# A routing pass folded into the unrolled feed-forward loop before it, and a regrouped head and tail of the state space stage

## What is computed

```python
y = groupnorm_complex(gate_loop(k, v, q, a), gn_scale, gn_bias) * silu(g)
y = (y @ Wo).real
x1 = layernorm(x + y, ln1_scale, ln1_bias)
out = x1 + (gelu(x1 @ W1 + b1) @ W2 + b2)
x = x + layernorm(out, ln2_scale, ln2_bias)
...
xn = layernorm(x)                              # router of layer 0
logits = xn @ gate_kernel                      # 64 experts
weights, selected = top_k(logits, 2)           # softmax over the two
sort_idx = argsort(selected.reshape(-1))       # rows of an expert go together
...
h = rmsnorm(layernorm(x))                      # layer 1
x_, z = split(h @ in_proj.T); xc = silu(causal_conv(x_))
dt, B, C = split(xc @ x_proj.T); dt = softplus(dt @ dt_proj.T + bias)
h_t = exp(dt * A) * h_(t-1) + (dt * xc) * B    # 512 channels x 16 states
x = x + ((sum over states of h_t * C) + D * xc) * silu(z) @ out_proj.T
```

## Time and profile before

| | us |
|---|---|
| median of 3 runs | 3226.64 (3224.76 to 3228.54) |
| the profiled execution | 3244.09 |
| its span, first to last instruction | 3242.3 |
| PE busy | 2644.0 (82%) |
| DVE busy | 1915.0 (59%) |
| POOL busy | 1381.8 (43%) |
| ACT busy | 1100.5 (34%) |

### The profile page before, as it was taken

One profiled execution on the slowest core, in us unless ns is written; L12 is line 12 of the kernel. 1 busy time (PEld: TensorE's weight loads), 2 busy tenths in 40 slices (PEclk: granted clock), 3 DMA queues, 4 the chain that ended last, 5 costly groups with the idle time before them and its releaser, 6 DMA issues. The chain is left out here.

```text
span 3242.3 us, 36222 instructions
## 1 busy us (share of the span) xinstructions
PE 2644.0 (82%) x12202; PEld 1809.4 (56%) x12202; DVE 1915.0 (59%) x3395; ACT 1100.5 (34%) x1766; POOL 1381.8 (43%) x865
## 2 busy tenths in 40 slices
PE   6772599754999999997488888988878776997998
PEld 3331366543999999996133333433433334666997
DVE  6999687362221221222789999999899994331211
ACT  6775122100111111111445545556465430221111
POOL 0000244335333333332059688697786851112332
PEclk9886799955999999998689998989989887998999
DMA  3000100012899999886200010110000101116996
GB/s 112 0 1 0 44 13 19 13 41 70 322 325 321 327 325 324 320 310 215 96 26 33 26 40 27 38 35 27 33 33 33 33 26 33 40 39 220 350 346 240
DMA packets 95181, 395.13 MB, mean 122 GB/s; under 512 B 21366, under 2 KB 48518, under 8 KB 72544
## 3 DMA queue, kind: packets, MB, share of 16 engines
q1 hardware_dynamic: 73472, 351.46, 30.9%
q0 software_dynamic: 21600, 42.37, 3.6%
HBM read 364.94 MB, written 39.29 MB: 125 GB/s over the span
## 5 line engine op out<-in xcount | busy, mean ns | idle before, releaser
L1327 POOL TENSOR_TENSOR ss_h<-ss_h,ss_cs 128x2048 f32<-128x2048 f32 x128 | 579.1, 4526 | 78.3 <-DVE ss_h L1693 70.3
L1407 PE MATMUL ss_y<-ss_h,all_ident 128*128 128x512 f32 x1024 | 525.8, 662 | 52.2 <-POOL ss_h L1327 52.0
L1176 DVE TENSOR_TENSOR experts_in<-experts_sil,experts_pU 128x512 f32<-128x512 f32 x176 | 120.9, 687 | 646.6 <-PE experts_pU L1120 612.8
L1693 DVE TENSOR_TENSOR_SCAN ss_h<-ss_da,ss_c_h,ss_dbu 128x512 f32<-128x512 f32 x384 | 470.7, 1268 | 7.4 <-ACT ss_da L1553 0.6
L1407 PEld LDWEIGHTS ss_y<-ss_h,all_ident 128*128 128x128 f32 x1024 | 215.3, 214 | 329.2 <-issue 263.1
L1553 ACT ACTIVATE ss_da<-ss_dt,ss_decay 128x512 f32<-128x512 f32 x512 | 326.7, 711 | 119.1 <-DVE ss_h L1693 69.0
L1686 DVE TENSOR_TENSOR ss_dbu<-ss_dtx,ss_bB 128x1024 f32<-128x1024 f32 x256 | 314.5, 1228 | 62.5 <-PE ss_bB L1397 36.0
L1120 PE MATMUL experts_pG<-experts_xt,experts_wa 128*128 128x128 f32 x2816 | 346.8, 277 | 0.9 <-DMA experts_wa<-in_w_all 0.9
L1120 PE MATMUL experts_pU<-experts_xt,experts_wa 128*128 128x128 f32 x2816 | 344.4, 276 | 0.0
L1129 PE MATMUL experts_pY<-experts_wa,experts_in 128*128 128x256 f32 x1408 | 332.7, 379 | 0.0
L1120 PEld LDWEIGHTS experts_pG<-experts_xt,experts_wa 128*128 128x128 f32 x2816 | 331.8, 193 | 1.3 <-ACT experts_xt L1146 1.1
(11 more groups left out here) (318 smaller groups left out, 3675.5 us busy)
## 6 DMA issues: line engine op xcount, KB each, us to landing
experts_wa<-in_w_all SPq DMA_DIRECT2D x176, 1536.0 KB
ss_cs<-ss_c_rows SPq DMA_DIRECT2D x64, 512.0 KB, 3.6
moe_rows<-route_xn SPq DMA_DIRECT2D x16, 512.0 KB
ss_h<-moe_ys SPq DMA_DIRECT2D x5, 1024.0 KB, 8.4
all_x<-in_x SPq DMA_DIRECT2D x8, 512.0 KB, 9.1
gf_xb<-in_x SPq DMA_DIRECT2D x8, 512.0 KB, 3.9
moe_rows<-all_x SPq DMA_DIRECT2D x8, 512.0 KB, 3.0
experts_xr<-moe_rows,moe_token POOLq DMA_INDIRECT x176
```

The source lines that it names most:

```text
L1176: nc.vector.tensor_tensor(IN[t.two][:].rearrange("p f t -> p (f t)"), SIL[t.two][:], pU[t.two][:], ALU.mult)\
L1327: pool.tensor_tensor(h[:], h[:], CS[q % 2][:, n % GROUP].unsqueeze(1).to_broadcast([P, CI, BT]), ALU.mult)\
L1407: mm = pe.matmul(y[:, c], ident[:], H[(b * N + n) % RING][:, c], start=(n == 0), stop=(n == N - 1))
L1693: ins = V.tensor_tensor_scan(H[(b * N + n) % RING][:, c], DA[(b * N + n) % AHEAD][:, c], DBU[:, c % 2], first, ALU.mult, ALU.add)
```

## The change

gate_ffn and the routing of layer 0 become one function, gate_ffn_route, unrolled in Python over NB + 3 = 11 steps in place of the hardware loops. In step i the first half of the feed-forward works on block i, the second half on block i-1, the router's rows, transposes and logits on block i-2, and its choice, ranks, slots and scatters on block i-3. The router's PSUM tiles pL and pR lie inside pW, the output of the W2 matmuls. The router's row statistics are found block by block. The closing part of the routing (number of tiles, owners, list gather, weights) is the same.

In state_space, block 0's Silu is taken chunk by chunk from PSUM with the bias, and x_proj takes each chunk as it comes; row_stats does its two inverse square roots in one chain over a two-row tile, and its call for blocks 1 to 7 stands before split_bc(0). At the end the last state's product is cut in two halves, PE adds it up chunk by chunk, DVE does skip and gate by chunk, and the output projection accumulates over the chunks in four regions of PSUM (LAST) that are free by then.

```diff
-def gate_ffn(nc, g, X, YS, SG, SUMS, ident):
...
+def gate_ffn_route(nc, g, X, YS, SG, SUMS, gate, r, ident):
...
+        pL, pR = (pW[:, 2 * n:2 * n + 2].rearrange("p t d -> p (t d)") for n in range(2))
+        pLt = pL[:, 0:TPB * E].rearrange("p (t e) -> p t e", e=E)
+        pRt = pR[:, 0:(TPB + 1) * E].rearrange("p (t e) -> p t e", e=E)
...
+        STEPS = range(NB + 3)
+        inside = lambda b: 0 <= b < NB
...
+                def enlist(b):
+                    wait(pool, "slots_ready", b + 1)
+                    for j in range(TPB):
+                        for k in range(K):
+                            pool.indirect_dma_start(lists, bass.IndirectOffsetOnAxis(ap=SL[b % 2][:, j, k:k + 1], axis=0),
+                                                    entry[:, b * TPB + j, k], None).then_inc(listed[b % 2], 16)
+
+                for i in STEPS:
+                    if inside(i):
+                        x1(i)
+                    if inside(i - 3):
+                        enlist(i - 3)
+                    if inside(i - 1):
+                        out(i - 1)
+                for h in range(2):
+                    pool.wait_ge(listed[h], LISTED * (NB // 2))
+                wait(pool, "list_done", 1)
...
+                def ffn_down(i):
+                    wait(pe, "h_free", i * FC + FC)
+                    wait(pe, "w2_read", i * TPB)
+                    wait(pe, "slots_ready", i - 1)
...
+                def route_turn(b):
+                    wait(pe, "rxn_done", b * TPB + TPB)
+                    wait(pe, "rxt_done", b * KD)
...
+                def logits(b):
+                    wait(pe, "rxt_done", b * KD + KD)
+                    wait(pe, "index_done", b)
+                    wait(pe, "w2_read", min(b + 2, NB) * TPB)
...
+                def ranks(b):
+                    wait(pe, "onehot_done", b * TPB + TPB)
+                    wait(pe, "slots_ready", b)
+                    wait(pe, "w2_read", min(b + 2, NB) * TPB)
...
+                for i in STEPS:
+                    if inside(i):
+                        wo(i)
+                    if i == 1:
+                        wait(pe, "loaded", LOADED)
+                        wait(pe, "gate_loaded", 16)
+                        wait(pe, "consts", 1)
+                    if inside(i - 3):
+                        ranks(i - 3)
+                    if inside(i - 1):
+                        ffn_up(i - 1)
+                    if inside(i - 2):
+                        route_turn(i - 2)
+                    if inside(i - 1):
+                        ffn_down(i - 1)
+                    if inside(i):
+                        turn(i)
+                    if inside(i - 2):
+                        logits(i - 2)
...
+                for i in STEPS:
+                    if inside(i - 1):
+                        gelu(i - 1)
+                    if inside(i - 2):
+                        copy_route(i - 2)
+                    if inside(i):
+                        copy_xt(i)
...
+                def route_rows(b):
+                    wait(dve, "out_done", b + 1)
+                    wait(dve, "rxt_raw", b - 1)
+                    if b > 1:
+                        dve.wait_ge(rows_stored[b % 2], 16 * (b // 2))
+                    normalise(lambda j: X[:, b * TPB + j], RXN[b % 2], "rxn_done", 1e-5)
...
+                z(0)
+                for i in STEPS:
+                    if inside(i - 3):
+                        choose(i - 3)
+                    if inside(i):
+                        first(i)
+                    if inside(i - 3):
+                        place(i - 3)
+                    if inside(i - 2):
+                        route_rows(i - 2)
+                    if inside(i + 1):
+                        z(i + 1)
+                    if inside(i - 1):
+                        second(i - 1)
...
+        LAST = [Q[:, 0:D], bB[:, 0:D], DBU[:, 0, 0:D], DBU[:, 1, 0:D]]
...
-                        wait(pool, "scanned", (b * N + n + 1) * 2)
+                        wait(pool, "scanned", (b * N + n + 1) * 2 - (1 if not prep and n == N - 1 else 0))
+                        if not prep and n == N - 1:
+                            break
...
-                gate(NB - 1)
+                last, row = H[(NB * N - 1) % RING], CS[(NB * GROUPS - 1) % 2][:, GROUP - 1].unsqueeze(1).to_broadcast([P, 2, BT])
+                pool.tensor_tensor(last[:, 0:2], last[:, 0:2], row, ALU.mult).then_inc(s["last_product"], 1)
+                wait(pool, "scanned", NB * N * 2)
+                pool.tensor_tensor(last[:, 2:4], last[:, 2:4], row, ALU.mult).then_inc(s["last_product"], 1)
...
-                    wait(pe, "xc_done", b + 1)
+                    wait(pe, "xc_done", b)
                     if b > 1:
                         wait(pe, "out_done", (b - 1) * 2)
-                    project(Q[:], WX, 0, XC[b % 2], CI).then_inc(s["xp_raw"], 1)
+                    for k in range(CI):
+                        if b == 0:
+                            wait(pe, "xb_done", k + 1)
+                        mm = pe.matmul(Q[:], WX[:, k], XC[b % 2][:, k], start=(k == 0), stop=(k == CI - 1))
+                    mm.then_inc(s["xp_raw"], 1)
...
-                add_up(NB - 1, N - 1)
-                out_part(NB - 1, 0)
-                out_part(NB - 1, 1)
+                for c in range(CI):
+                    wait(pe, "last_product", c // 2 + 1)
+                    pe.matmul(y[:, c], ident[:], H[(NB * N - 1) % RING][:, c], start=False, stop=True).then_inc(s["last_sum"], 1)
+                wait(pe, "z_done", NB * CI)
+                wait(pe, "dbu_done", NB * N * 2)
+                wait(pe, "scanned", NB * N * 2)
+                for c in range(CI):
+                    wait(pe, "yz_done", (NB - 1) * CI + c + 1)
+                    for j in range(TPB):
+                        mm = pe.matmul(LAST[j], DTX[(NB - 1) % 2][:, c, j * P:(j + 1) * P], WO[:, c], start=(c == 0), stop=(c == CI - 1))
+                        if c == CI - 1:
+                            mm.then_inc(s["out_raw"], 1)
...
-                    A_(XC[b % 2][:, c], bank(b, c), ACT.Identity, bias=conv_b[:, c:c + 1]).then_inc(s["xb_done"], 1)
+                    A_(XC[b % 2][:, c], bank(b, c), ACT.Silu if b == 0 else ACT.Identity, bias=conv_b[:, c:c + 1])\
+                        .then_inc(s["xb_done"], 1)
...
-                    A_(XC[b % 2][:], XC[b % 2][:], ACT.Silu).then_inc(s["xc_done"], 1)
+                    if b > 0:
+                        A_(XC[b % 2][:], XC[b % 2][:], ACT.Silu).then_inc(s["xc_done"], 1)
...
-                    v, d, q, t = var[:, a:b], rstd[:, a:b], rms[:, a:b], tmp[:, a:b]
-                    norm_stats(nc, pre, lambda j: X[:, a + j], stats[:, a:b], mv[:, a:b], d, t, 1e-5, var=v)
...
+                    v, r, w, d, t = VARS[:, :, a:b], ROOTS[:, :, a:b], TMP2[:, :, a:b], rstd[:, a:b], tmp[:, a:b]
...
+                    pre.mark(V.tensor_scalar(v[:, 0], mv[:, a:b, 1], 1.0, 1e-5, ALU.mult, ALU.add))
+                    pre.link(V.tensor_scalar(v[:, 1], mv[:, a:b, 1], 1e-30, None, ALU.max))
+                    rsqrt(nc, pre, r, v, w)
+                    pre.link(V.tensor_tensor(t, v[:, 1], r[:, 1], ALU.mult))
+                    pre.link(V.tensor_tensor(t, t, r[:, 0], ALU.mult))
+                    pre.link(V.tensor_scalar(t, t, 1e-5, None, ALU.add))
+                    pre.link(V.reciprocal(d, t))
+                    pre.link(V.tensor_tensor(d, d, r[:, 0], ALU.mult))
...
                     add_experts(b)
+                row_stats(1, NB - 1)
                 split_bc(0)
-                row_stats(1, NB - 1)
...
-                add_skip(NB - 1)
-                add_out(NB - 1, 0)
-                add_out(NB - 1, 1)
+                b = NB - 1
+                wait(dve, "zs_done", NB)
+                for c in range(CI + 1):
+                    if c < CI:
+                        wait(dve, "last_sum", c + 1)
+                        V.scalar_tensor_tensor(DTX[b % 2][:, c], XC[b % 2][:, c], skip[:, c:c + 1], y[:, c], ALU.mult, ALU.add)\
+                            .then_inc(s["skip_done"], 1)
+                    if c > 0:
+                        wait(dve, "skip_done", b * CI + c)
+                        V.tensor_tensor(DTX[b % 2][:, c - 1], DTX[b % 2][:, c - 1], ZS[:, c - 1], ALU.mult).then_inc(s["yz_done"], 1)
+                for j in range(TPB):
+                    wait(dve, "out_raw", b * 2 + j + 1)
+                    V.tensor_tensor(X[:, b * TPB + j], X[:, b * TPB + j], LAST[j], ALU.add).then_inc(s["out_done"], 1)
...
-            gate_ffn(nc, g, X, YS, SG, SUMS, ident)
-        route(nc, "route0", X, g["router0"], r0, ident)
+            gate_ffn_route(nc, g, X, YS, SG, SUMS, g["router0"], r0, ident)
```

More of the change, by code:

```diff
@@ L1202, in state_space @@
         stats, mv = m_.sb("stats", [P, NT, 6]), m_.sb("mv", [P, NT, 2])
[L1203 removed]
+        rstd, tmp, shift = (m_.sb(n, [P, NT]) for n in ("rstd", "tmp", "shift"))
```

(10 more changed lines are left out.)

503 lines of the change are left out of this document (293 added, 210 removed).

## The result

| | before | after |
|---|---|---|
| median of 20 runs each, us | 3228.23 (3224.22 to 3233.33) | 3234.45 (3229.82 to 3238.0) |
| the profiled execution | 3244.09 | 3231.63 |
| its span | 3242.3 | 3229.8 |
| mean granted clock | 0.897 | 0.904 |

What follows compares the result with a forecast made beforehand. PE bounds the old gate_ffn (32.14 of 33.00 us); a coupled chain sets the folded cycle. Fold +28.4, state space head -20.6, tail -13.3: -5.5 us, so 3221 us, range 3185 to 3250.

Steps and rivals of the forecast that it cites:

- the 150.1 us of the old tail: Old route stage, from the end of the last W2 matmul to the end of the last scatter: 150.1 us, removed.
- a 3 us charge on the new kernel: Folded loop: stalls as instruction streams grow, half of one 6.58 us stall seen in the route stage; bounds 0 and 39.
- 95.6 us less: After block 7's W2 end: 54.5 us to the last scatter in place of 150.1 us.
- the prediction's own signs of being wrong: Whole forecast: wrong if the cycle is off by more than 2 us, or "remote" takes more than 10.
- the cycle: Folded loop, W2 end to next W2 end: second, choose, first, place with route_rows, route_turn with ffn_down; 50.5 us against 33.0.
- The rival of the bursts: Folded loop: each of six scatter bursts costs DVE 6.58 us, 36 us more in all, 3257 us; chance 0.18.
- The first cycle: First of the folded loop's seven cycles: no choose, but first runs in out's shadow; 47.5 us.
- The new tail: Folded routing, from block 7's W2 end to the end of the last scatters: 54.5 us.
- the fold: gate_ffn and routing as one: loop 120.0 us more, ending 95.6 less, semaphores +1, stalls 3; +28.4 us.
- The port case: Folded loop: POOL's passes hold DVE back less, cycle 41.7 us if none waited; 3159 us, in part 3190; chance 0.20.
- The tail: End of state space, last scan to last addition: PE sums, skip and gate by chunk; 13.3 us less.
- the rival that half of the head's gain is handed back: State space: scan starts earlier, but C rows or block 1's preparation come late; half of 20.6 lost, 3231 us; chance 0.10.

Runs made afterwards that it cites:

- experiment 1: The kernel before, unchanged, run again for a second profile: 3227.36 us.
- experiment 11: The kernel before with layer 0's scatters put off until the last block's slots are there, with eight slot buffers in place of two: 3298.59 us.
- experiment 10: The changed kernel, unchanged, on the chip where before took 3245.39 us: 3232.54 us, ratio 0.996.
- experiment 8: The changed kernel with ffn_up ahead of ranks, route_turn inside ffn_down, and POOL's out starting behind the one-hot rows: 3161.44 us.
- experiment 2: The kernel before with only the changed gate_ffn_route, its state space stage kept: 3261.01 us, ratio 1.0103.
- experiment 7: The changed kernel with POOL's passes cut from three to two in x1 and three to one in out, factors missing from the result: 3193.66 us.
- Experiments 4 to 6: The changed kernel with PE's order edited: ffn_up ahead of ranks alone 3238.22 us, route_turn inside ffn_down alone 3225.98 us, both 3175.61 us.
- experiment 3: The kernel before with only the changed state space stage, head and tail: 3196.78 us, ratio 0.9903.
- experiment 6: The changed kernel with both PE order edits, ffn_up ahead of ranks and route_turn inside ffn_down: 3175.61 us.

## Why the prediction was wrong, step by step

**The step that failed is the 150.1 us of the old tail.** It was read off one execution that ran 17.5 us over the median, and the difference of stages was then put on the median as it stood. In an execution of the median's length the stretch takes 132.7 us (experiment 1). None of the 20 runs of before that the result rests on took over 3233.33 us, while in the two slow groups all 24 took 3240.8 to 3256.5: with its 3244.09 us and its stalls the first profile looks like one of those; where it ran isn't recorded. The rows that spoke against the 150.1 us were at hand: the earlier trace rows show DVE idle for 6.58 us with its input done, in that very stage. They were used for a 3 us charge on the new kernel and for a rival (bursts that stop the other engines), and not taken off the old one. With 132.7 in place of 150.1 the same working gives -5.5 + 17.4 = +11.9 us, slower, and "95.6 us less" becomes 132.7 - 54.5 = 78.2. None of the prediction's own signs of being wrong pointed at this term: the cycle came within 2 us, and "remote" took nothing.

**The rival of the bursts had the right stalls and the wrong kernel.** Late scatters make the stalls go (experiment 11), but on the chip that shows them the changed kernel took no longer, and no idle time in its gate_ffn_route was ended by "remote" (experiment 10). The 3 us taken for them were 0. Most of its bursts lie under ffn_down, where DVE has little to do; that this is why they cost nothing isn't shown. One reading of the earlier trace rows was off: not all of ACT's 19.46 us was a stall, for the transposes that ACT waited for ended at 696.96, 10.1 us before it went on at 707.05:

```profile
695.05 1.91 PE L831 MATMUL route_pT<-all_ident,route_xn 128*128 128x128 f32 x8
```

Nor is "remote" by itself a stall: in experiment 8 ACT's wait for route_turn is given as "remote" in four of the cycles, as in this row, and those cycles are as long as the others.

```profile
518.20 1.08 ACT L751 ACTIVATE gf_rxt<-gf_pT 128x512 f32<-128x512 f32 x2 [18.43 <-remote]
```

The Trainium skill (Runtime: NRT & Kernel Launch, Instruction fetch mechanics) says that straight code is fetched ahead and that the cost of it is mostly hidden. For gate_ffn_route the trace agrees: no stall beyond the waits of the chain in its 49.3 us.

**The cycle was right in its make-up and 1.2 us too long.** 7.0 + 8.4 + 7.6 + 11.4 + 15.0 = 49.4 against 7.3 + 8.9 + 7.6 + 11.7 + 15.0. The forecast of 9 to 10 us idle PE before ranks met 9.09. The first cycle was 46.7 (47.5), the last 48.5 (48.9), the seven together 342.3 (348.9). The new tail was 53.4 (54.5). So the fold costs 113.4 - 79.3 + 1.2 = 35.3 us by the traces, 33.6 by the runs of experiment 2; forecast were 28.4, which is 17.4 too little by the old tail and 10.5 too much by the new loop (6.6), its tail (1.1) and the stalls (3), less 0.2. That the two errors are of opposite sign is luck: the whole forecast is only 11.7 us off (-5.5 for +6.2), less than the one term.

**The port case was rightly put aside.** Experiments 7 and 8 show what DVE's operations wait for: with fewer passes, or with the same passes elsewhere, choose takes 4.3 and 3.4 us, near the 4.6 and 3.5 expected. That the one-hot L846 would wait as well, as the forecast assumed, is not seen: it took 0.87 us behind out's end and with POOL idle alike, and no row has it in the middle of a pass. The one sentence of the Trainium skill used here (SBUF — State Buffer, Who interferes with whom: an operation of DVE with two SBUF inputs or in a two-port mode contends with GpSimd, and the one that comes later is blocked) fits the 1.06 us of L835 in experiment 7 and the 4.79 of L843 in after.

**What the prediction did not see is that the cycle was a matter of order.** Its chain takes the places of route_turn and ranks, ahead of the feed-forward's matmuls, as given, and it didn't ask which waits came from data and which only from a place in PE's queue. Experiments 4 to 6 show that 58.8 us hang on the two places together.

**Head and tail.** The tail was 13.7 us shorter in after (13.3), but 11.5 in experiment 3: the forecast had PE's sums end late, as in the earlier trace rows (12.82 us), and in after they took 10.48. With the premise as it was, the term is 1.8 us too large, and that after meets it is luck. The first DBU came 70.3 us into the stage in after and 69.9 in experiment 3 (69.9). The rival that half of the head's gain is handed back was met in small: by the end of the last scan the stage is 1130.4 us old in after, 1127.1 in experiment 3, and 1148.2 and 1147.5 in the first two profiles of before, so 17 to 21 us are left, where 20.6 were forecast. Against the second profile of before, 2.7 us of this are waits for PE's B rows, which the first profile has too (experiment 3). Another 3.3 us between after and experiment 3, whose state space code is the same, were not traced to a cause; 2.2 of them come back in the tail. Head, scan and tail together are 30.8 us shorter in after than in the second profile of before, 31.9 in experiment 3 and 30.7 by its runs; forecast were 33.9.

**The sum as it should have been:** +35.3 for the fold, -17.1 for head and scan, -13.7 for the tail: +4.5, against a measured +6.2 and a difference of spans of +5.6 between after and the second profile of before. The way there from the forecast: -5.5, plus 17.4 for the old tail, minus 10.5 for the new loop, its tail and the stalls, plus 3.1 that head, scan and tail gave less.

## What to carry to other kernels

Set the profiled execution against the median before any subtraction, and where it is longer, look for the excess in the stage that the change removes: an engine that stands idle though its input is done may belong to that execution alone, and not to the median from which the stage is taken. When a loop is folded over several engines, mark each wait as data or as place in a queue; here two waits of the second kind, each hidden behind the other, made a fold that costs 34 us out of one that gains 23 (from block 0's W2 end to the last scatter it is 395.7 us in after and 361.6 in the second profile of before, 338.8 in experiment 6 and 326.2 in experiment 8). And test such pairs together: in a full cycle each alone gave nothing.

## What the runs showed of the hardware

- The same program takes 3227 us in one group and 3245 to 3250 in the two others, each on one chip. In the profiles at 3244 us (the first, and one of the third group) DVE stands idle for 3.8 to 6.6 us at a time beside bursts of indirect scatters from POOL, where it is 1.5 to 2.2 us in the profile at 3226 us, and ACT once for 10.1 us after its input was done; from the last W2 matmul to the last scatter it is 150.1 and 149.2 us, against 132.7. With the scatters behind the work the stalls are gone; their cause is open.
- PE loses clock to short idle stretches as well. 48 W2 matmuls take 10.63 us at a granted clock of 1.00 where PE idled for under 1 us. After 14 us of W1's matmuls, 3 of ranks and 2.60 of idle time, all at 1.00, they take 12.28, with 0.55 in the first 3.8 us, and after 4.0 us of idle time 12.1 to 13.3.
- While a POOL pass runs, a small operation of DVE of the waiting kind lasts until the pass ends: 2.21 us for a 128x4 integer operation that takes 0.17 without, 4.79 for four one-hot rows that take 0.74 (experiment 7).
